# Scores and outputs of an attention take turns in two accumulator banks, the normalised rows get a buffer of their own, and the order of all work is written anew

## The reference

```python
# layer 0: causal self attention, 16 heads of 32; then attention on the context
# (32 heads), then a gated network with weights and activations quantised in blocks of 32
x = x + attn(layernorm(x)); x = x + xattn(layernorm(x), ctx); x = x + ffn(layernorm(x))
# layer 1: a state scan (32 heads x 128 states), cross attention with 16 heads of 32,
# then a mixture of 8 low-rank experts
q = (x @ Wq.T + bq).reshape(B, N, H, D).transpose(0, 2, 1, 3)
scores = jnp.einsum('bhqd,bhkd->bhqk', q, k) * SCALE
scores = jnp.where(mask[None, None], NEG_INF, scores)      # causal
attn = jax.nn.softmax(scores, axis=-1)
out = jnp.einsum('bhqk,bhkd->bhqd', attn, v)
return out.transpose(0, 2, 1, 3).reshape(B, N, C) @ Wo.T + bo
```

## Time and profile before

| | |
|---|---|
| time, median of 3 runs | 1620.25 us (1616.87 to 1622.1) |
| span of the profiled execution, first to last instruction | 1615.7 us |
| busy: PE, DVE, ACT, POOL | 1374.8, 1347.9, 1038.7, 423.9 us |
| mean granted clock of PE | 0.937 |

### The profile page before, as it was taken

How to read it: one execution, slowest core, us unless ns; L and a number is a source line. 1 busy time by engine, 2 the same in 40 slices (tenths; PEclk the granted TensorE clock), 3 DMA queues, 4 the chain that set the end, 5 groups by cost and what they waited for, 6 DMA issues and landing times.

```text
span 1615.7 us, 31163 instructions
## 1 busy us (share of the span) xinstructions
PE 1374.8 (85%) x12080; PEld 729.4 (45%) x12080; DVE 1347.9 (83%) x2015; ACT 1038.7 (64%) x1884; POOL 423.9 (26%) x488
## 2 busy tenths in 40 slices
PE   3778888879899999889978777879999999999986
PEld 2443445334445453444443333436455555555542
DVE  6989989979879888887898899978698888978743
ACT  3244365465673865756585768985799788989430
POOL 1432041132341522322331240241222313122210
PEclk9687979799999999999999988889999999999987
DMA  6313112200201111002130003111020211101020
GB/s 227 93 53 93 52 49 66 74 14 1 74 14 40 36 40 41 21 22 54 51 100 28 1 1 138 27 27 44 2 70 2 69 34 38 40 5 44 4 77 26
DMA packets 54194, 76.38 MB, mean 47 GB/s; under 512 B 8353, under 2 KB 23713, under 8 KB 53537
## 3 DMA queue, kind: packets, MB, share of 16 engines
q1 hardware_dynamic: 54048, 74.40, 16.3%
HBM read 39.24 MB, written 9.44 MB: 30 GB/s over the span
## 4 chain that ended last, share of the span: by engine, by line
PE 48%; DVE 29%; ACT 10%; issue 7%; POOL 3%; DMA 1%; SPq 0%; ACTq 0%; DVEq 0%; POOLq 0%
PE bank L193 17%; DVE mix_NM L1058 4%; PE bank L1158 4%; PE bank L526 3%; PE bank L534 2%; PE bank L514 2%; DVE ssm_HS L1518 2%; PE bank L971 2%; DVE ffn_m L1112 2%; PE bank L487 2%; DVE ffn_Z L1122 2%; PE bank L549 2%; PE bank L931 2%; PE bank L956 2%; DVE ffn_room L1130 1%
## 5 line engine op out<-in xcount | busy, mean ns | idle before, releaser
L1031 ACT ACTIVATE mix_P<-bank 128x512 f32<-128x512 f32 x256 | 142.2, 603 | 52.6 <-PE bank L956 50.7
L1058 DVE TENSOR_REDUCE mix_NM<-bank 128x2 f32<-128x512 f32 x256 | 164.4, 683 | 10.5 <-PE bank L931 9.8
L714 POOL TENSOR_SCALAR_AFFINE_SELECT cross_P<-cross_P 128x256 f32<-128x256 f32 x128 | 87.9, 696 | 280.3 <-ACT cross_P L628 280.0
L1276 POOL TENSOR_TENSOR ffn_room<-ffn_room 128x512 f32<-128x512 f32 x64 | 90.9, 1421 | 266.9 <-ACT ffn_room L1215 170.0
L1518 DVE TENSOR_TENSOR_SCAN ssm_HS<-ssm_DA,ssm_DD 128x1024 f32<-128x1024 f32 x64 | 150.2, 2347 | 11.4 <-ACT ssm_DD L1469 6.6
L714 POOL TENSOR_SCALAR_AFFINE_SELECT attn_P<-attn_P 128x256 f32<-128x256 f32 x128 | 86.3, 686 | 247.0 <-ACT attn_P L628 246.9
L1466 ACT ACTIVATE ssm_DA<-ssm_Z,A_T 128x255 f32<-128x255 f32 x256 | 110.8, 498 | 2.4 <-DVE ssm_HS L1518 2.1
L628 ACT ACTIVATE attn_P<-bank 128x384 f32<-128x384 f32 x128 | 63.8, 498 | 64.7 <-PE bank L515 64.2
L628 ACT ACTIVATE cross_P<-bank 128x384 f32<-128x384 f32 x128 | 62.7, 490 | 52.3 <-PE bank L515 51.7
L1524 DVE TENSOR_TENSOR ssm_HS<-ssm_HS,ssm_CS 128x1024 f32<-128x1024 f32 x64 | 80.7, 1261 | 0.9
L1441 ACT ACTIVATE ssm_Z<-bank 128x512 f32<-128x512 f32 x128 | 72.2, 598 | 13.6 <-PE bank L1354 12.9
(11 more groups left out here) (408 smaller groups left out, 4072.9 us busy)
## 6 DMA issues: line engine op xcount, KB each, us to landing
attn_stack<-attn_P SPq DMA_DIRECT2D x96, 128.0 KB, 2.4
cross_stack<-cross_P SPq DMA_DIRECT2D x96, 128.0 KB, 2.5
ffn_room<-f_gate SPq DMA_DIRECT2D x4, 1024.0 KB, 5.9
XR<-x SPq DMA_DIRECT2D x8, 512.0 KB, 6.4
ffn_room<-f_up SPq DMA_DIRECT2D x4, 1024.0 KB, 5.5
ffn_room<-f_down SPq DMA_DIRECT2D x4, 1024.0 KB, 5.5
x_mid<-XR SPq DMA_DIRECT2D x8, 512.0 KB, 3.0
XR<-x_mid SPq DMA_DIRECT2D x8, 512.0 KB, 3.8
```

What stands on the lines that cost most here:

```text
L714: nc.gpsimd.affine_select(out=diagonal, in_=diagonal, compare_op=ALU.is_ge, fill=0.0, base=0, pattern=[[0, 2], [1, P]], channel_multiplier ...
L1031: nc.scalar.activation(self.p[h % 8], bank[b4[h % 2]][:, :], ACT.Exp, scale=HD2 ** -0.5).then_inc(s["p_ready"], 1)
L1058: nc.vector.tensor_reduce(self.nm[:, t, 16 * i + 2 * g:16 * i + 2 * g + 2], bank[b4[u % 3]][:, :].rearrange("p (c k) -> p c k", c=2), AX.X ...
L1276: nc.gpsimd.tensor_tensor(self.inter[q % 2][:, 512 * (g % 2):512 * (g % 2) + 512], self.sg[g % 2], self.up[g % 2], ALU.mult).then_inc(s["i ...
```

## The change

Three edits in `Attention`, and new strings of turns. First, the scores of the heads and the outputs of four heads each alternate between `b[0]` and `b[1]` in the order in which PE writes them, instead of a bank each. Second, `oc` moves from the buffer of `xn` to that of `xt`, and the split outputs (`ot`) move to the last slots of `p`; `xn` is then free for the next batch as soon as it has been transposed, and its scaling becomes a stream of ACT of its own, `act_norm`, in place of the first step of `act`. Third, ACT copies the outputs of four heads one head earlier. The turns of all five engines are new. No instruction is added or dropped.

```diff
-                self.oc = self.xn[:, :, :].rearrange("p t d -> p (t d)").rearrange("p (c k) -> p c k", c=DC)
+                halves = lambda t_: Split(*(t_[:, i * DC * S:(i + 1) * DC * S].rearrange("p (c k) -> p c k", c=DC)
+                                            for i in range(2)))
+                self.xt = halves(both[:, :])
+                self.oc = both[:, :].bitcast(F32).rearrange("p (c k) -> p c k", c=DC)
+                self.ot = halves(self.space[:, 2 * DC * S:3 * DC * S].bitcast(F16))
+                turns, self.scores_bank, self.out_bank = 0, [], []
+                for h in range(H1 + 3):
+                    if h < H1:
+                        self.scores_bank.append(banks[turns % 2])
+                        turns += 1
+                    if h >= 6 and h % 4 == 2:
+                        self.out_bank.append(banks[turns % 2])
+                        turns += 1
...
-                        b = self.b[0]
+                        b = self.scores_bank[h]
...
-                        o, sums = self.b[1], self.b[2]
+                        o, sums = self.out_bank[c], self.b[2]
...
-            def act(self, act, n):
+            def act_norm(self, act, n):
                 yield
                 if n:
-                    act.wait_ge(self.ot_ready, 2 * n)
+                    act.wait_ge(self.xt_ps, TT * n)
                 if n == B:
                     act.wait_ge(*hidden_over)
                 self.norm.act_scale(act, self.x(n), n)
-                for t in range(TT):
-                    yield
+
+            def act(self, act, n):
+                for t in range(TT):
+                    yield
+                    if n and t == 0:
+                        act.wait_ge(self.ot_ready, 2 * n)
...
-                    if h >= 8 and h % 4 == 0:
+                    if h >= 7 and h % 4 == 3:
                         yield
-                        c = h // 4 - 2
+                        c = (h - 7) // 4
                         act.wait_ge(self.o_ps, DC * n + c + 1)
-                        nc.scalar.copy(self.oc[:, c, :], bank[self.b[1]][:, 0:S]).then_inc(self.o_ready, 1)
+                        nc.scalar.copy(self.oc[:, c, :], bank[self.out_bank[c]][:, 0:S]).then_inc(self.o_ready, 1)
...
-        "daggppbbgggpgppggggggggbbbbbbbbbbbbgbggggggaggggbgbbbbgggbbabbcgggdggggdggbbbbbbbbbbbbbdddgddggg"
+        "pabpbggggggggggagpggdpggpggggggggggbbbbbbbbbbbbgbaggggggggggbgbbbbgbbcbbggggadgdggggbbbbbbbbbbbb"
```

More of the change, by code:

```diff
@@ new lines @@
+        "aaaaaacccaaaaaaaaacaaaaaaaaaaaaaaacaaaaaaacaaaaaaaaaaaaaaacaaacaaaaaaaaaaaaaaaaaaaaaaabaaaaaabab"
+        "aaaaaaaabaaaaaababccbaabaaaaaaabcabaaabaaacabaababaabaaaaaaaabaaaabaaaaabaaabacaaaabaaaaaaaabaaa"
+        "aaaaaabcabbcbbbcbbaaabaabaaaabbabaaaaababababacbbbacbbababbbbbaaaaaaacacbababbabababaaababaabbab"
+        "aabbaaababbaaabababaaabaaaaaaabaabbbbaabcaabababbabaabaaabaabbaabacbbaabbabbbabbcabbabcaaaaaaaab"
+        "abbbababaaabaaadbadbddbabadbdababdbadbdbdabaaabaaddaadbdaaabaaaddbaaabbabbdbaddbbbddddaabddaabad"
@@ L566, in pe @@
                         cols = slice(t * P, (t + 1) * P)
-                        last = product(bank[b][:, :], [(self.xt.view(lambda t_: t_[:, c, cols]),
+                        last = product(bank[b][:, :], [(self.ot.view(lambda t_: t_[:, c, cols]),
                                                         self.wo.view(lambda t_: t_[:, c, :]))],
@@ L619, in act @@
                 nc.scalar.mul(self.nq.high[:, :], bank[self.b[2]][0:32, 0:S], 1 / RANGE).then_inc(self.nqh_ready, 1)
-                for h in range(H1 + 5):
+                for h in range(H1 + 4):
                     if h < H1:
@@ L627, in act @@
                             act.wait_ge(self.pv_done, (m - 8) // 4 + 1)
-                        nc.scalar.activation(self.p[h % 8][:, :], bank[self.b[0]][:, 0:S + P], ACT.Exp,
+                        nc.scalar.activation(self.p[h % 8][:, :], bank[self.scores_bank[h]][:, 0:S + P], ACT.Exp,
                                              scale=HD1 ** -0.5).then_inc(self.p_ready, 1)
-                    if h >= 8 and h % 4 == 0:
+                    if h >= 7 and h % 4 == 3:
                         yield
-                        c = h // 4 - 2
+                        c = (h - 7) // 4
                         act.wait_ge(self.o_ps, DC * n + c + 1)
-                        nc.scalar.copy(self.oc[:, c, :], bank[self.b[1]][:, 0:S]).then_inc(self.o_ready, 1)
+                        nc.scalar.copy(self.oc[:, c, :], bank[self.out_bank[c]][:, 0:S]).then_inc(self.o_ready, 1)
                 for half in range(2):
@@ L639, in act @@
                     act.wait_ge(self.on_ready, 2 * n + half + 1)
-                    nc.scalar.copy(self.xt.high[:, two, :], self.oc[:, two, :]).then_inc(self.oh_ready, 1)
+                    nc.scalar.copy(self.ot.high[:, two, :], self.oc[:, two, :]).then_inc(self.oh_ready, 1)
             def dve(self, dve, own, n):
@@ L690, in dve @@
                     dve.wait_ge(self.oh_ready, 2 * n + half + 1)
-                    nc.vector.tensor_tensor(self.xt.low[:, two, :], self.oc[:, two, :], self.xt.high[:, two, :],
+                    nc.vector.tensor_tensor(self.ot.low[:, two, :], self.oc[:, two, :], self.ot.high[:, two, :],
                                             ALU.subtract).then_inc(self.ot_ready, 1)
@@ L1929, in _ @@
                              in_turn(lambda i: weights_a.act(act, i), items_a),
-                             in_turn(lambda i: weights_f.act(act, i), items_f))
+                             in_turn(lambda i: weights_f.act(act, i), items_f),
+                             in_turn(lambda n: attn.act_norm(act, n)),
+                             in_turn(lambda n: cross.act_norm(act, B + n)))
             @block.vector
```

115 lines of the change are left out of this document (55 added, 60 removed).

## The result

The changed kernel takes 1646.03 us (median of 4 runs, 1645.4 to 1646.22), the kernel before on the same chip 1620.01 us (median of 4). The ratio is 1.0153, with a 95% interval of 1.0129 to 1.0176: 26 us slower, where I had forecast 12 us faster, with a range up to 1623. The profiled execution of the changed kernel has a span of 1644.0 us.

What follows compares the result with a forecast made beforehand. Bounds: DVE to 430 and from 850 to 1100 us, PE from 430 to 850 and 1100 to 1500, dependences at the end. 1615.7 less 12.5 (13.5 gained, 1 off) gives 1603.2; plus 4.5, 1608 us; range 1594 to 1623.

Steps and rivals of the forecast that it cites:

- the new order at the start: Start of the kernel: first row maximum stands behind 23.5 us more DVE work, done earlier and missing later; costed at nothing.
- Slower: Rival, chance 0.13: early stretch runs out of DVE filler; with 20 of the 23.5 us back as idle time, 1627 us.
- units remain until the fourth batch in both orders: Argument against the rival Slower: quantising units are still left as DVE filler until the fourth batch, before and after.
- orders that meet new small waits: Whole kernel: an allowance of 1 us taken off the gain for the new turns.
- Two banks for the scores: Attention heads: next head's scores are made during the exponential; 8 to 10 us less for a bare attention of sixteen heads.
- The sum of 13.5 us: Gain from shorter waits over five stretches: 4.5, 2.5, 1, 3 and 2.5 us, bounds 0 and 26.2.
- DVE's waits at its reciprocal before 430 us: Sign of being right: DVE's wait at the reciprocal of the sums, 10.6 us in three times, falls under 7 us.
- The copy of the outputs: Heads: after each group of outputs, a bubble of about 0.4 us, three in a batch, 1.2 us per bare attention.
- The first batch's heads: Sign of being right: heads of the first attention batch take 16 to 18 us instead of 22.7.
- No change: Rival, chance 0.2: heads quicker, but POOL's masks and other stages' products take up the time; 1616 to 1624 us.
- The buffer and the scaling stream: Next batch's scaling in both layers: covered by other waits, costed at nothing; at most 1.52 us for a batch if uncovered.
- The difference between span and median: Whole kernel: 4.5 us between profiled span and median of the runs, added to the forecast span.

Runs made afterwards that it cites:

- short passes: All edits, five of seven long DVE passes per quantising unit on 64 instead of 2048 columns: 1586.27 us with old turns, 1611.21 with new (0.9779 and 0.9939).
- the mixture with the quantising taken back: The changed kernel with new turns for all but the quantising steps, which stand where the old turns have them: 1649.86 us, 1.0175 to the kernel before.
- the first measurement: First of two measurements of all edits with the old turns, against the kernel before: 1614.66 us, 0.9985 (0.9954 to 1.0015).

## Why the prediction was wrong

**The step that failed** is the one on the new order at the start: "DVE is the leading engine there and only does this work earlier [...] I cost it at nothing: the cover is that the same passes are missing later". The count behind it was right: the first row maxima came 23 us later. The cover does not exist. With the new turns up to 100 us alone, the passes are missing later, but DVE has no other work ready then, since it waits for the sums of the attention that started late (71.0 us of DVE work from 100 to 200 us instead of 94.4), and the kernel takes 1.16% more, some 19 us. In the change more passes fill part of that gap (85.5 us), and the attentions stay as late. Taking away 98.9 us of the quantising gives 34 us. So passes ahead of the first attention cost most of their length, some 19 to 21 us for 23.5, while many others only fill gaps. That it is the passes, and not the other early turns, rests on the delay of the reciprocals with short passes (24.4 us down to 8.6); the mixture with the quantising taken back did not get the time back, so what the other early turns cost stays open.

Two things led me there. I took the fullest engine of the stretch, DVE with 378 of 430 us, for the one that sets the time. And I looked at the passes in DVE's order alone. PE takes its own instructions in order as well: in the new turns the transposes of the second unit stand ahead of half of the first batch's q and k and all of its v, and PE was idle 19.5 us for them. It had 4.6 us to spare at the first maxima (scores done at 74.5 us, DVE there at 79.1), so had DVE come earlier, this wait would have been the next limit. The transposes of the units (the row of the releaser in the view of that line, PE and its weight loads together) waited 2.4 us with the old turns and 57.6 us with the new:

```profile
L829 PE MATMUL bank<-ident,ffn_room x192: 219/219/315, 36.2 to 367.5; 128*128 128x128 bf16 x192
...
  DVE ffn_room L817: 57.6, 7
```

The Trainium skill ("PSUM — Partial Sum Buffer", the section on engine and sequencer instructions) says that matrix products start and complete in program order. By that rule, this wait holds up everything behind it, and the trace agrees: the other half of q and k starts only at 58.85 us. The rival *Slower* had the stretch and the amount that comes back (20 us), and I gave it 0.13; it named the mixing stage as what DVE would wait for, where the longest wait was for the first attention's sums, and its 1627 still counted on 13 us of gain from the edits. I had put "units remain until the fourth batch in both orders" against it. That they remain said nothing on whether they would be needed as filler.

**The late part** was not in the prediction at all. I had taken 1 us for "orders that meet new small waits"; the turns from 700 to 870 us cost 0.5 to 0.85%, 7 to 14 us.

**Two banks for the scores.** The mechanism was right, and PE's waits for the exponentials fell as forecast, even in the changed kernel: 3.1 us, none listed, 0.7, 2.4 and 1.4 us in the five stretches, 7.6 in all where they were 29.1. The size was off. The sum of 13.5 us measured 2 us (interval -1 to 5.5; 7.5 at most in the first measurement). DVE's waits at its reciprocal before 430 us fell from 10.6 to 7.7 us in the change, where I had said under 7. In the kernel with all edits and the old turns other waits of the heads have grown. From 0 to 430 us PE waits there:

```profile
PE bank L538 <- POOL attn_P L730: 12.4, 7, 4.2
...
PE bank L526 <- ACT attn_X L650: 7.3, 8, 1.5
...
PE bank L526 <- ACT attn_P L644: 1.4, 5, 0.4
```

The copy of the outputs, which I had priced at 0.4 us three times a batch, costs 21.7 us over the five stretches (7.3 + 5.0 + 1.6 + 6.1 + 1.7), about the 19 us which that price makes for 16 batches, and it is paid in the busy attentions too, where I had counted only bare ones. And POOL's masks have 12.4 us where they had 8.5. The first batch's heads, which I expected in 16 to 18 us, took 22.3 in the change (scores at 92.18, last sums done at 114.47):

```profile
92.18 0.37 PE L526 MATMUL bank<-attn_stack 128*128 128x256 f16 x1 [3.58 <-issue]
...
98.81 1.51 PE L538 MATMUL bank<-attn_P,attn_V 128*32 128x256 f32 x16 [2.50 <-POOL attn_P L730]
...
113.64 0.83 PE L546 MATMUL bank<-attn_P,ones_of_four 128*32 128x256 f32 x16
```

In these heads PE waits for the masks (L730) where it waited for the exponential. The outcome of the edits is that of the rival *No change*. Its cause, "the masks of POOL [...] take up the time", holds for 3.9 us from 0 to 430 us; the larger part is the copy. What the Trainium skill tells of a kernel in which double-buffered accumulators gave no further gain ("TensorE: Matmul & The Clock Gate", the section on oscillation) came out nearer than my sum.

**The buffer and the scaling stream** were costed at nothing, and the run without the two banks shows nothing (1.0009). As forecast, the next batch's transposes wait for DVE's last addition and not for the scaling:

```profile
125.95 1.06 PE L423 MATMUL bank<-ident,attn_XN 128*128 128x128 f32 x8 [0.89 <-DVE XR L714]
```

**The difference between span and median** was put at 4.5 us; in every run of these experiments the time is 2.0 to 3.4 us above the span, and the rest is the spread between executions.

## What to carry to other kernels

Work without deadlines that fills an engine's gaps is free only in the gaps. Before you pull it ahead of the first item of a pipeline, ask what the engine will do at the place it leaves, and count it nearly in full if the answer is that it waits for that item. The fullest engine of a stretch need not set its time: shorten its work in a kernel and see how much comes back, here a third. And when work moves in the order of one engine, look up in the order of each other engine what now stands behind the step that consumes it, since a wait there holds up everything in the queue.

## What I had not expected of the hardware

The same program differs from one execution to the next by about 1%, and the granted clock goes with it. All edits with the old turns had a span of 1608.1 us at a mean granted clock of 0.950, and of 1624.7 us at 0.934, on one chip. The two profiled executions of this program, on two chips, part in the first attention (windows of the heads, first measurement and second):

```profile
68.00:92.00 24.00, 15.01 (x180) 8.72 (x184) 20.76 (x21) 9.38 (x21) 16.26 (x18) 0.75 0.36 117
```

```profile
68.00:92.00 24.00, 16.27 (x168) 9.26 (x172) 18.44 (x18) 8.65 (x21) 16.18 (x18) 0.64 0.36 117
```

With the same instructions PE had a mean granted clock of 0.75 in one and 0.64 in the other, so it spent more of the stretch at the lower of its two levels in the second, and the third reciprocal stood 6.0 us later there (241.1 against 235.1). That the clock alone makes this difference is not shown. But it is as large as the gain that the edits could have, which is why 12 executions did not settle edits of that size.
